# One step of a two-graph pipeline reordered on three engines, and one add moved in the closing

## The chip, the cores and the metric

The kernel runs on one core of one Trainium2 chip. The metric is device microseconds of one execution; times quoted for a kernel are the median of several executions.

## The reference

One layer of a gated graph network on 64 graphs of 128 nodes with 256 features, in float32:

```
mask[d]  = (adj == d),  d = 1..4                 # adj holds 0 and 1 here
agg[d]   = mask[d] / (rowsum(mask[d]) + 1e-8) @ hid
out      = relu(concat_d(agg[d]) @ Wd.T + bd)
r        = sigmoid(out @ Wri.T + bri + hid @ Wrh.T + brh)
z        = sigmoid(out @ Wzi.T + bzi + hid @ Wzh.T + bzh)
n        = tanh(out @ Wni.T + bni + r * (hid @ Wnh.T + bnh))
o        = (1 - z) * n + z * hid
result   = (o - mean(o)) / sqrt(var(o) + 1e-5) * gamma + beta
```

## The kernel before, in words

The 64 graphs are worked in 32 pairs, numbered from 0. Step i does the label sums (y, p and t banks) of pair i, the gates of pairs i-2 and i-3, and the normalisation of pair i-4. Steps 0 and 1 are `head()`, step 2 and step 3 are written out (`plain_step()` and `step()`), and from step 4 on every step is `fast_step()`, in which the products y = x Wd are also done with seven block products instead of eight (A.. and S.. are blocks of x and their sums, B.. and T.. blocks of the weights). Step 4 is the first of these, `n == 1`, with its own branches; it works on the fifth pair, number 4, and prepares the x of the sixth, number 5. Behind step 31 each engine has a `tail()`, the closing.

Every float32 operand of TensorE is split in a high part, rounded by ScalarE (`x_hi`, `y_hi`, `o_hi`), and a rest, taken by GpSimd or VectorE (`x_lo`, `y_lo`, `o_lo`), and a product is three passes. Each engine has its own program, written out by hand; an engine works its rows in that order and waits at semaphores (`wait_ge`). So an instruction that waits holds up all that stands behind it on its engine.

The path of a pair's x: a DMA on SyncE's queue (`load_x`, L316) brings it into `x_f`, GpSimd adds and subtracts four sum blocks (`sum_blocks`, three instructions, L1729, L1731 and L1735, which count `xsum_ready` up), ScalarE rounds all eight blocks to `x_hi` (L1013 in a fast step), and GpSimd takes `x_lo` (L1848).

What stands around the change in step 4:

- TensorE: the products of y: A11 B11, S2 T2, A12 B21, S3 T3 and S1 T1, then A22 T4 (it waits for `u3y_ready`), then S4 B22 (it waits for `y22_ready`), then the gate products. The counts of labels (`counted`, L438, eight tiny matmuls) stand at the end of step 3 for pair 4, and from step 5 on between S1 T1 and A22 T4.
- ScalarE: copies `u2_y` out of the bank (L1007), rounds x (L1013), rounds `y_hi` (L1017), copies `u3_y` (L1021), takes the sigmoid of r (L1026; it waits for `result_ready`, the last row of VectorE's normalisation), and so on to `gamma` (L1040), the bias of the next gate product.
- GpSimd: at the end of step 3 `o_lo` (L1787), then the two rows of the root 1/sqrt(var + eps) (L1827, L1829), then, at the start of step 4, the sums of pair 5.
- VectorE: L1410 adds up the mix, L1465 takes the rest of weight block T4, L1476 (two rows) scales and shifts with the root (`rstd_ready`), L1480 takes a `y_lo`, L1484 adds `u3_y` and counts `y22_ready` up.

In the closing VectorE centres the mix (`centre`, L1546) and then adds C12 (L1647, `c12_ready`), for which ScalarE's next `gamma` waits (L1116); TensorE's product S1 T1 of the closing waits for that `gamma` and for GpSimd's `o_lo` (L1905).

Of the kernel before, what the change touches and what calls it, by code (L numbers as in the profile page):

```python
# [4 lines left out]
GRAPHS, N, H, D = 64, 128, 256, 4  # L5
# [7 lines left out]
XRING = 4  # L13
# [25 lines left out]
def gnn_kernel(nc, x, xT, adjT, wdT, wgT, bd, vectors, out):  # L39
    f32, f32r, bf16, i32 = mybir.dt.float32, mybir.dt.float32r, mybir.dt.bfloat16, mybir.dt.int32  # L40
    ALU, ACT = mybir.AluOpType, mybir.ActivationFunctionType

    ctx = ExitStack()
    with ctx:
# [29 lines left out]
        x_f = sb("x_f", [128, 2, 8, N])  # L74
        x_hi = sb("x_hi", [128, XRING, 8, N], f32r)
# [100 lines left out]
        xhi_ready = sem("xhi_ready")  # L176
        xlo0_ready = sem("xlo0_ready")
        xlo_ready = sem("xlo_ready")
        xsum_ready = sem("xsum_ready")
# [107 lines left out]
        def has_pair(k):  # L287
            return 0 <= k < PAIRS
# [119 lines left out]
        def _(pe):  # L408
# [25 lines left out]
            def counted(k):  # L434
                for g in range(2):
                    halves = masks[:, k % 2, g, :, :].bitcast(bf16).rearrange("n d (m t) -> n d m t", t=2)
                    for d in range(D):
                        last = nc.tensor.matmul(t_bank[:, g * D + d:g * D + d + 1], halves[:, d, :, 1],  # L438
                                                ones_bf[:, :], start=True, stop=True)
                last.then_inc(count_done, 1)  # L440
# [90 lines left out]
            def step(i, up):  # L531
# [11 lines left out]
                def count(k):  # L543

                    pe.wait_ge(masks_ready, up(D * (k + 1), D))
                    pe.wait_ge(olo_ready, up(k - 1))
                    counted(k)
# [91 lines left out]
                pe.wait_ge(c22_ready, up(q + 1))  # L639
                product(gamma, S4, B22).then_inc(p3_done, 1)  # L640
                p_part(i, 1, False)
                count(i + 1)

            def fast_step(i, up):

                q, n, slot = i - LAG_GATES, i - YS + 1, i % XRING

                def y_product(dst, left, w, first=False):
                    return three_passes(dst[:, :], x_hi[:, slot, left, :], x_lo[:, slot, left, :], *wd_block(w), first=first)

                def product(k, dst, left, w):
                    three_passes(dst[:, 0:GATE], x_hi[:, k % XRING, left, :], x_lo[:, k % XRING, left, :],
                                 wx_hi[:, w, :], wx_lo[:, w, :])
                    return three_passes(dst[:, 128:512], o_hi[:, k % 2, left - 1, :], o_lo[:, k % 2, left - 1, :],
                                        wo_hi[:, w, :], wo_lo[:, w, :])

                pe.wait_ge(xlo_ready, up(i - 1))

                if n == 1:
                    pe.wait_ge(ylo_ready[0], 2 * YS)  # L660
                else:
                    pe.wait_ge(yl21_ready, up(n - 1))
                y_product(y_alpha, A11, B11, True).then_inc(yp1_done, 1)
                if n == 1:
                    pe.wait_ge(alpha_loaded, up(q + 1))
                    pe.wait_ge(olo_ready, up(q + 1))
                    product(q, alpha, A11, B11).then_inc(p1_done, 1)
                else:

                    pe.wait_ge(u3_ready, up(q - 1))  # L670
                    product(q - 1, alpha, A22, T4).then_inc(p4_done, 1)
                    pe.wait_ge(yl11_ready, up(n - 1))
                    pe.wait_ge(yl12_ready, up(n - 1))
                    pe.wait_ge(out_ready, up(2 * i - 1, 2))
                    p_products(i - 1, 1, False)
                pe.wait_ge(y11_seeded, up(n))
                if n == 1:
                    pe.wait_ge(wdt_ready, 3)
                y_product(y_alpha, S2, T2).then_inc(yp6_done, 1)
                if n >= 2:  # L680
                    pe.wait_ge(c22_ready, up(q))
                    product(q - 1, gamma, S4, B22).then_inc(p3_done, 1)
                y_product(beta, A12, B21).then_inc(yp2_done, 1)
                pe.wait_ge(p_scaled, up(4 * i, 4))
                p_products(i - 1, 1, True)
                pe.wait_ge(u2y_ready, up(n))
                y_product(y_alpha, S3, T3).then_inc(yp7_done, 1)
                if n == 1:
                    pe.wait_ge(ylo_ready[1], 2 * YS)
                else:  # L690
                    pe.wait_ge(y12_ready, up(n - 1))
                y_product(y_gamma, S1, T1, True).then_inc(yp5_done, 1)
                if n >= 2:
                    pe.wait_ge(alpha_loaded, up(q + 1))
                    pe.wait_ge(olo_ready, up(q + 1))
                    product(q, alpha, A11, B11).then_inc(p1_done, 1)
                    pe.wait_ge(masks_ready, up(D * (i + 1), D))
                    counted(i)
                pe.wait_ge(u3y_ready, up(n))
                if n == 1:  # L700
                    pe.wait_ge(wdt_ready, 4)
                y_product(y_alpha, A22, T4).then_inc(yp4_done, 1)
                pe.wait_ge(y22_ready, up(n))
                y_product(y_gamma, S4, B22).then_inc(yp3_done, 1)
                pe.wait_ge(beta_seeded, up(q + 1))
                pe.wait_ge(oslo_ready, up(q))
                product(q, alpha, S2, T2).then_inc(p6_done, 1)
                pe.wait_ge(out_ready, up(2 * i, 2))
                pe.wait_ge(ratio_ready, up(i + 1))
                transposes()  # L710
                pe.wait_ge(gamma_loaded, up(q + 1))
                product(q, gamma, S1, T1).then_inc(p5_done, 1)
                pe.wait_ge(yl21_ready, up(n))
                pe.wait_ge(yl22_ready, up(n))
                p_products(i, 0, False)
                pe.wait_ge(u2_ready, up(q))
                product(q, alpha, S3, T3).then_inc(p7_done, 1)
                product(q, beta, A12, B21).then_inc(p2_done, 1)
                pe.wait_ge(p_scaled, up(4 * i + 2, 4))
                p_products(i, 0, True)  # L720
# [65 lines left out]
        def _(act):  # L786
# [189 lines left out]
            def fast_step(i, up):  # L976
                q, m, n = i - LAG_GATES, i - LAG_MIX, i - YS + 1

                def scale(k, g):
# [3 lines left out]
                    for b in range(2):  # L983
                        nc.scalar.activation(p_bank[:, b * H:(b + 1) * H], p_bank[:, b * H:(b + 1) * H], ACT.Copy,  # L984
                                             scale=ratio[:, k % 2, g, b:b + 1]).then_inc(p_scaled, 1)

                if n == 1:

                    act.wait_ge(wdt_sum, 4)
                    act.wait_ge(y_done[1], 2 * YS)  # L990
                    nc.scalar.activation(wd_block(T4)[0], wd_sum_of[T4], ACT.Copy).then_inc(wdt_hi_ready, 1)
# [13 lines left out]
                if n >= 2:  # L1005
                    act.wait_ge(yl12_ready, up(n - 1))
                nc.scalar.activation(u2_y[:, :], y_alpha[:, :], ACT.Copy).then_inc(u2y_ready, 1)  # L1007
                if has_pair(i + 1):
                    k = i + 1
                    act.wait_ge(xsum_ready, up(3 * k, 3))  # L1010

                    act.wait_ge(p3_done, up(i - 2))
                    nc.scalar.activation(x_hi[:, k % XRING, :, :], x_f[:, k % 2, :, :], ACT.Copy).then_inc(xhi_ready, 1)  # L1013
                act.wait_ge(yp2_done, up(n))

                act.wait_ge(p_done, up(2 * i, 2))
# [2 lines left out]
                if n >= 2:  # L1019
                    act.wait_ge(yl22_ready, up(n - 1))  # L1020
                nc.scalar.activation(u3_y[:, :], y_alpha[:, :], ACT.Copy).then_inc(u3y_ready, 1)  # L1021
                act.wait_ge(c11_ready, up(m + 1))
                act.wait_ge(c21_ready, up(m + 1))

# [149 lines left out]
        def _(dve):  # L1174
# [366 lines left out]
            def tail():  # L1541
                last = PAIRS - 1

                def centre(k, g):
                    dve.wait_ge(mv_ready, 2 * k + 2)
                    nc.vector.scalar_tensor_tensor(mix[:, g * H:(g + 1) * H], mix[:, g * H:(g + 1) * H],  # L1546
                                                   mean_var[:, g, 0:1], vec_rows[:, gamma_rows],
                                                   ALU.subtract, ALU.mult).then_inc(scaled_ready, 1)
# [91 lines left out]

                mixed(last - 3)
                moments(last - 3)
                centre(last - 3, 0)
                centre(last - 3, 1)
                dve.wait_ge(p3_done, last - 1)
                dve.wait_ge(u2_ready, last - 2)
                nc.vector.tensor_tensor(c_sb[:, ODD, 1, :], gamma[:, :], u2_sb[:, :], ALU.add).then_inc(c12_ready, 1)  # L1647
                sum_labels(1)

                dve.wait_ge(y12_ready, YPAIRS)  # L1650
# [59 lines left out]
        def _(pool):  # L1710
# [65 lines left out]
            def step(i, up):  # L1776
# [13 lines left out]
                if i == HEAD:  # L1790
# [32 lines left out]
                                        from_n[:, :].rearrange("p (g f) -> p g f", g=2), ALU.mult)\  # L1823
                    .then_inc(zpart_ready, 1)
                split_o_sums()
                pool.wait_ge(mv_ready, 2)
                nc.gpsimd.tensor_tensor(var_eps[:, :], mean_var[:, :, 1], ln_eps[:, :], ALU.add).then_inc(ve_ready, 1)  # L1827
                pool.wait_ge(ve_ready, 1)
# [1 line left out]

            def fast_step(i, up):
                m, j, n = i - LAG_MIX, i - LAG_NORM, i - YS + 1
                if n == 1:
                    sum_blocks(i + 1, up, 16 * ((i + 1) // 2 + 1))
                if n >= 2:
                    pool.wait_ge(mv_ready, up(2 * j + 2, 2))
                    nc.gpsimd.tensor_tensor(var_eps[:, :], mean_var[:, :, 1], ln_eps[:, :], ALU.add).then_inc(ve_ready, 1)  # L1837
# [127 lines left out]
```

## Time and profile before

| | us |
|---|---|
| median of 3 executions (510.44 to 510.72) | 510.55 |
| the profiled execution, its own time | 512.22 |
| its span, first to last instruction | 510.4 |
| TensorE busy (96% of the span) | 492.4 |
| VectorE busy (84%) | 429.1 |
| ScalarE busy (83%) | 421.9 |
| GpSimd busy (73%) | 370.4 |
| an x_f load, issue to landing, median | 2.6 |

The views name engines PE (TensorE), ACT (ScalarE), DVE (VectorE), POOL (GpSimd) and SPq (the DMA queue of SyncE). TensorE is busy in nearly the whole span, so what counts is where it stands still and at which clock it works; the mean granted clock is 0.988 of full speed.

### The profile page before, as it was taken

Reading aid. Unit: us, or ns where it says so; the run is one execution under the profiler, and the core shown is the slowest. Engines: PE = TensorE matmul, PEld = TensorE weight load, DVE = VectorE, ACT = ScalarE, POOL = GpSimd, SP = SyncE. Lnnn points to the kernel's source line nnn. Section 1 sums busy time; section 2 is a strip of 40 time slices with the busy share of each in tenths; the row PEclk is TensorE's granted clock in tenths of the full one; section 3 lists DMA queues with packets and bytes.
Section 4 is the critical chain, followed back from the end, with each engine's and each line's share of the span. In section 5 each row is a group of like instructions: output and inputs, shape, how many; then the busy total and the mean of one; then the engine's idle time right before and its main releaser. Section 6 shows DMA issues by size and latency. Waiting matters only on the chain.

```text
span 510.4 us, 10652 instructions
## 1 busy us (share of the span) xinstructions
PE 492.4 (96%) x2951; PEld 447.7 (88%) x2951; DVE 429.1 (84%) x1077; ACT 421.9 (83%) x819; POOL 370.4 (73%) x369
## 2 busy tenths in 40 slices
PE   8999979999999999999999999999999999999992
PEld 4789769999999999999999999999999999999892
DVE  4899968888888988888898888889888888988877
ACT  5878758888888898888989888888988889897772
POOL 2889776777887777788777778877777887775535
PEclk9999979999999999999999999999999999999997
DMA  8310222111222212122221212222111222110111
GB/s 274 127 54 1 83 83 73 53 51 44 74 74 72 72 51 51 41 72 72 72 72 51 51 41 72 72 72 72 51 51 41 72 72 72 51 41 22 42 42 62
DMA packets 20261, 33.42 MB, mean 65 GB/s; under 512 B 2256, under 2 KB 6992, under 8 KB 20240
## 3 DMA queue, kind: packets, MB, share of 16 engines
q1 hardware_dynamic: 19872, 32.38, 20.4%
q10 hardware_dynamic: 288, 0.52, 0.3%
q0 software_dynamic: 80, 0.26, 0.1%
q8 instruction: 9, 0.15, 0.1%
q14 instruction: 12, 0.10, 0.1%
HBM read 24.77 MB, written 8.39 MB: 65 GB/s over the span
## 4 chain that ended last, share of the span: by engine, by line
PE 86%; POOL 6%; DVE 4%; issue 1%; DMA 1%; ACT 1%; SPq 0%; POOLq 0%; ACTq 0%; DVEq 0%
PE y_bank L412 25%; PE alpha L412 24%; PE gamma L412 12%; PE p_bank L449 11%; PE beta L412 10%; PE t_bank L457 3%; DMA adj_in<-in_adjT 1%; PE t_bank L438 1%; POOL x_lo L1782 1%; POOL wo_lo L1739 1%; DVE y_lo L1203 1%; POOL x_rows L1743 1%; POOL x_f L1731 0%; DVE wd_lo L1209 0%; DVE mix L1410 0%
## 5 line engine op out<-in xcount | busy, mean ns | idle before, releaser
L449 PE MATMUL p_bank<-y_hi,masks 128*128 128x256 f32 x256 | 66.9, 283 | 1.1 <-DVE y_lo L1203 0.4
L449 PE MATMUL p_bank<-y_lo,masks 128*128 128x256 f32 x256 | 66.5, 282 | 0.0
L1848 POOL TENSOR_TENSOR x_lo<-x_f,x_hi 128x1024 fp32r<-128x1024 f32 x27 | 65.1, 2410 | 1.2 <-ACT x_hi L1013 1.2
L1851 POOL TENSOR_TENSOR y_lo<-shared,y_hi 128x512 fp32r<-128x512 f32 x28 | 36.6, 1309 | 25.2 <-ACT y_hi L1036 25.2
L1837 POOL TENSOR_TENSOR var_eps<-mean_var,ln_eps 128x2 f32<-128x2 f32 x27 | 5.3, 196 | 66.2 <-DVE mean_var L1455 66.2
L449 PEld LDWEIGHTS p_bank<-y_hi,masks 128*128 128x128 f32 x256 | 48.1, 188 | 4.4 <-issue 1.4
L412 PE MATMUL y_bank<-wd_hi,x_hi 128*128 128x512 f32 x112 | 47.2, 422 | 3.3 <-ACT shared L1021 3.3
L449 PEld LDWEIGHTS p_bank<-y_lo,masks 128*128 128x128 f32 x256 | 48.2, 188 | 1.3
L984 ACT ACTIVATE p_bank<-p_bank,ratio 128x256 f32<-128x256 f32 x112 | 45.3, 448 | 0.3 <-PE p_bank L449 0.3
L412 PE MATMUL y_bank<-wd_lo,x_hi 128*128 128x512 f32 x112 | 44.8, 400 | 0.0
L412 PE MATMUL y_bank<-wd_hi,x_lo 128*128 128x512 f32 x112 | 44.6, 398 | 0.0
L412 PE MATMUL alpha<-wx_hi,x_hi 128*128 128x384 f32 x122 | 41.4, 339 | 0.1
L412 PE MATMUL alpha<-wx_hi,x_lo 128*128 128x384 f32 x122 | 41.4, 340 | 0.0
L412 PE MATMUL alpha<-wo_hi,o_hi 128*128 128x384 f32 x122 | 41.4, 339 | 0.0
L412 PE MATMUL alpha<-wo_hi,o_lo 128*128 128x384 f32 x122 | 41.4, 339 | 0.0
L412 PE MATMUL alpha<-wx_lo,x_hi 128*128 128x384 f32 x122 | 41.2, 338 | 0.0
L412 PE MATMUL alpha<-wo_lo,o_hi 128*128 128x384 f32 x122 | 41.2, 337 | 0.0
L1859 POOL TENSOR_TENSOR shared<-x_rows,shared 128x512 f32<-128x512 f32 x28 | 36.3, 1295 | 3.8 <-ACT shared L1045 3.8
L1426 DVE SCALAR_TENSOR_TENSOR out_rows<-p_bank,rcount,bd_rows 128x256 f32<-128x256 f32 x56 | 27.1, 483 | 13.3 <-PE p_bank L449 11.5
L1863 POOL TENSOR_TENSOR shared<-shared 128x512 f32<-128x512 f32 x28 | 36.2, 1295 | 2.2
L1866 POOL TENSOR_TENSOR y_lo<-shared,y_hi 128x512 fp32r<-128x512 f32 x28 | 36.6, 1309 | 0.0
L1843 POOL TENSOR_TENSOR o_lo<-o_sums,o_hi 128x512 fp32r<-128x512 f32 x27 | 35.0, 1297 | 0.0
(315 smaller groups left out, 1796.2 us busy)
## 6 DMA issues: line engine op xcount, KB each, us to landing
x_f<-in_xT SPq DMA_DIRECT2D x32, 256.0 KB, 2.6
x_rows<-in_x SPq DMA_DIRECT2D x32, 256.0 KB, 2.7
out<-shared SPq DMA_DIRECT2D x31, 256.0 KB, 2.0
adj_in<-in_adjT SPq DMA_DIRECT2D x32, 128.0 KB, 2.1
shared<-in_wgT SPq DMA_DIRECT2D x2, 576.0 KB, 6.6
shared<-in_wdT ACTq DMA_DIRECT2D x2, 256.0 KB, 5.4
vec_rows<-in_vectors SPq DMA_DIRECT2D x1, 512.0 KB, 7.0
shared<-in_wgT SPq DMA_DIRECT2D x2, 192.0 KB, 7.8
```

The lines of the kernel that those rows point to most:

```text
L412: done = nc.tensor.matmul(dst, m, w, start=(first and t == 0), stop=(last and t == 2), skip_group_check=inside)
L449: last = nc.tensor.matmul(p_bank[:, b * H:(b + 1) * H], masks[:, k % 2, g, d, :], part[:, g, d * H:(d + 1) * H], start=first, stop=(part i ...
L457: last = nc.tensor.transpose(t_bank[:, (2 * g + c) * N:(2 * g + c + 1) * N], out_rows[:, g, c * N:(c + 1) * N], ident[:, :])
L984: nc.scalar.activation(p_bank[:, b * H:(b + 1) * H], p_bank[:, b * H:(b + 1) * H], ACT.Copy, scale=ratio[:, k % 2, g, b:b + 1]).then_inc(p ...
L1426: nc.vector.scalar_tensor_tensor(out_rows[:, g, :], p_bank[:, 0:H], rcount[:, k % 2, g, 1:2], bd_rows[:, :], ALU.mult, ALU.add).then_inc(h ...
L1837: nc.gpsimd.tensor_tensor(var_eps[:, :], mean_var[:, :, 1], ln_eps[:, :], ALU.add).then_inc(ve_ready, 1)
L1843: nc.gpsimd.tensor_tensor(*split_lo(o_lo[:, i % 2, 3:7, :], o_sums[:, 1:5, :], o_hi[:, i % 2, 3:7, :]))\
L1848: nc.gpsimd.tensor_tensor(*split_lo(x_lo[:, k % XRING, :, :], x_f[:, k % 2, :, :], x_hi[:, k % XRING, :, :])).then_inc(xlo_ready, 1)
L1851: nc.gpsimd.tensor_tensor(*split_lo(y_lo[:, EVEN, half(1)], u3_y[:, :], y_hi[:, EVEN, half(1)]))\
L1859: nc.gpsimd.tensor_tensor(from_n[:, :], x_rows[:, m % 2, :, :].rearrange("p g f -> p (g f)"), n_sb[:, :], ALU.subtract).then_inc(from_read ...
L1863: nc.gpsimd.tensor_tensor(z_part[:, :].rearrange("p (g f) -> p g f", g=2), rz_sb[:, :, 1, :], from_n[:, :].rearrange("p (g f) -> p g f", g ...
L1866: nc.gpsimd.tensor_tensor(*split_lo(y_lo[:, ODD, half(1)], u2_y[:, :], y_hi[:, ODD, half(1)]))\
```

## The change

In step 4 four things move. ScalarE rounds the x of pair 5 behind the copy to `u3_y` instead of behind the copy to `u2_y`. GpSimd makes the sums of pair 5 at the end of step 3, ahead of the two rows of the root, instead of at the start of step 4 behind them, and waits for the same load (48 is what the formula before gives). TensorE counts the labels of pair 4 between S1 T1 and A22 T4 of step 4 instead of at the end of step 3, as all later steps do, and the wait for `olo_ready` that stood ahead of that count goes. In the closing VectorE adds C12 ahead of the two centring rows. No instruction is added or taken out.

```diff
 # TensorE, step() (step 3)
                 p_part(i, 1, False)
-                count(i + 1)
 # TensorE, fast_step()
-                    pe.wait_ge(masks_ready, up(D * (i + 1), D))
-                    counted(i)
+                pe.wait_ge(masks_ready, up(D * (i + 1), D))
+                counted(i)
                 pe.wait_ge(u3y_ready, up(n))
 # ScalarE, fast_step()
+                def x_high():
+                    k = i + 1
+                    act.wait_ge(xsum_ready, up(3 * k, 3))
+
+                    act.wait_ge(p3_done, up(i - 2))
+                    nc.scalar.activation(x_hi[:, k % XRING, :, :], x_f[:, k % 2, :, :], ACT.Copy).then_inc(xhi_ready, 1)
...
                 nc.scalar.activation(u2_y[:, :], y_alpha[:, :], ACT.Copy).then_inc(u2y_ready, 1)
-                if has_pair(i + 1):
-                    k = i + 1
-                    act.wait_ge(xsum_ready, up(3 * k, 3))
-
-                    act.wait_ge(p3_done, up(i - 2))
-                    nc.scalar.activation(x_hi[:, k % XRING, :, :], x_f[:, k % 2, :, :], ACT.Copy).then_inc(xhi_ready, 1)
+                if n >= 2 and has_pair(i + 1):
+                    x_high()
...
                 nc.scalar.activation(u3_y[:, :], y_alpha[:, :], ACT.Copy).then_inc(u3y_ready, 1)
+                if n == 1:
+
+                    x_high()
 # VectorE, tail()
-                centre(last - 3, 0)
-                centre(last - 3, 1)
                 dve.wait_ge(p3_done, last - 1)
                 dve.wait_ge(u2_ready, last - 2)
                 nc.vector.tensor_tensor(c_sb[:, ODD, 1, :], gamma[:, :], u2_sb[:, :], ALU.add).then_inc(c12_ready, 1)
+                centre(last - 3, 0)
+                centre(last - 3, 1)
 # GpSimd, step() (step 3)
                 split_o_sums()
+
+                sum_blocks(5, up, 48)
                 pool.wait_ge(mv_ready, 2)
 # GpSimd, fast_step()
-                if n == 1:
-                    sum_blocks(i + 1, up, 16 * ((i + 1) // 2 + 1))
```

ScalarE's rows of step 4 before, from the copy to `u2_y` (first row) over the rounding of x (second) and the copy to `u3_y` (fourth):

```order
L1007 ACTIVATE shared<-y_bank 128x512
L1013 ACTIVATE x_hi<-x_f 128x1024
L1017 ACTIVATE y_hi<-beta 128x512
L1021 ACTIVATE shared<-y_bank 128x512
L1026 ACTIVATE mix<-shared 128x512
```

The same stretch of the changed kernel, whose lines have other numbers:

```order
L1013 ACTIVATE shared<-y_bank 128x512
L1019 ACTIVATE y_hi<-beta 128x512
L1023 ACTIVATE shared<-y_bank 128x512
L991 ACTIVATE x_hi<-x_f 128x1024
L1031 ACTIVATE mix<-shared 128x512
```

The rounding of x now stands behind the copy to `u3_y` and ahead of the sigmoid of r.

GpSimd's rows at the seam of steps 3 and 4 before: `o_lo`, the two rows of the root, the three rows of the sums of pair 5, and the rest `x_lo` of pair 5:

```order
L1787 TENSOR_TENSOR o_lo<-o_sums,o_hi 128x512
L1827 TENSOR_TENSOR var_eps<-mean_var,ln_eps 128x2
L1829 TENSOR_TENSOR rstd<-var_eps,power 128x2
L1729 TENSOR_TENSOR x_f<-x_f 128x128
L1731 TENSOR_TENSOR x_f<-x_f 128x256
L1735 TENSOR_TENSOR x_f<-x_f 128x128
L1848 TENSOR_TENSOR x_lo<-x_f,x_hi 128x1024
```

The same stretch of the changed kernel:

```order
L1792 TENSOR_TENSOR o_lo<-o_sums,o_hi 128x512
L1734 TENSOR_TENSOR x_f<-x_f 128x128
L1736 TENSOR_TENSOR x_f<-x_f 128x256
L1740 TENSOR_TENSOR x_f<-x_f 128x128
L1834 TENSOR_TENSOR var_eps<-mean_var,ln_eps 128x2
L1836 TENSOR_TENSOR rstd<-var_eps,power 128x2
L1853 TENSOR_TENSOR x_lo<-x_f,x_hi 128x1024
```

The root is now behind the three sums, and `x_lo` is behind the root as before.

On TensorE the difference is one row, the count of pair 4, at the seam of steps 3 and 4 and at its new place in step 4, between S1 T1 (weights `wdt`) and A22 T4 (weights `wd`):

```order
 L449 MATMUL p_bank<-y_lo,masks 128x256
-L438 MATMUL t_bank<-ones_bf,masks 128x1 x8
 L412 MATMUL y_bank<-wd_hi,x_hi 128x512
 L412 MATMUL y_bank<-wd_hi,x_lo 128x512
@@ -282,4 +281,5 @@
 L412 MATMUL y_bank<-wdt_hi,x_lo 128x512
 L412 MATMUL y_bank<-wdt_lo,x_hi 128x512
+L438 MATMUL t_bank<-ones_bf,masks 128x1 x8
 L412 MATMUL y_bank<-wd_hi,x_hi 128x512
 L412 MATMUL y_bank<-wd_hi,x_lo 128x512
```

All other rows of TensorE keep their order.

## Rows read from the trace of the kernel before

**Rows 1.** Waits of TensorE, whole execution: total us, times, longest.

```profile
PE y_bank L412 <- ACT shared L1021: 3.3, 1, 3.3
PE gamma L412 <- POOL o_lo L1905: 0.6, 1, 0.6
```

**Rows 2.** Windows: length, busy us by engine (PE PEld DVE ACT POOL), granted clock, DMA.

```profile
94.00:109.00 15.00, 15.00 (x93) 13.85 (x92) 12.86 (x34) 13.05 (x26) 11.36 (x12) 1.00 0.21 62
67.00:68.00 1.00, 0.00 (x0) 0.00 (x0) 0.00 (x0) 1.00 (x2) 0.01 (x1) 0.97 0.89 260
```

**Rows 3.** Timeline of TensorE, step 4: start, us, form [idle before <- releaser].

```profile
59.87 0.34 PE L438 MATMUL t_bank<-ones_bf,masks 128*128 128x1 bf16 x8 [0.84 <-DVE o_lo L1350]
...
61.09 0.44 PE L412 MATMUL alpha<-wx_hi,x_hi 128*128 128x384 f32 x1
...
64.57 0.39 PE L412 MATMUL y_bank<-wdt_lo,x_hi 128*128 128x512 f32 x1
...
68.94 0.79 PE L412 MATMUL y_bank<-wd_hi,x_hi 128*128 128x512 f32 x1 [3.27 <-ACT shared L1021]
...
70.38 0.63 PE L412 MATMUL y_bank<-wd_hi,x_hi 128*128 128x512 f32 x1
...
78.69 0.39 PE L412 MATMUL y_bank<-wd_hi,x_hi 128*128 128x512 f32 x1
```

**Rows 4.** Timeline of ScalarE, steps 3 and 4.

```profile
60.44 0.60 ACT L974 ACTIVATE alpha<-vec_rows 128x512 f32<-128x512 f32 x1
...
66.85 1.06 ACT L1013 ACTIVATE x_hi<-x_f 128x1024 fp32r<-128x1024 f32 x1 [3.11 <-POOL x_f L1735]
...
68.29 0.59 ACT L1021 ACTIVATE shared<-y_bank 128x512 f32<-128x512 f32 x1
68.77 0.60 ACT L1026 ACTIVATE mix<-shared 128x512 f32<-128x512 f32 x1
...
71.32 0.60 ACT L1040 ACTIVATE gamma<-bias_step 128x512 f32<-128x512 f32 x1
```

**Rows 5.** Timeline of GpSimd at the seam of steps 3 and 4.

```profile
60.73 1.29 POOL L1787 TENSOR_TENSOR o_lo<-o_sums,o_hi 128x512 fp32r<-128x512 f32 x1
63.73 0.19 POOL L1827 TENSOR_TENSOR var_eps<-mean_var,ln_eps 128x2 f32<-128x2 f32 x1 [1.72 <-DVE mean_var L1320]
64.00 0.72 POOL L1829 TENSOR_TENSOR rstd<-var_eps,power 128x2 f32<-128x2 f32 x1
...
66.36 0.46 POOL L1735 TENSOR_TENSOR x_f<-x_f 128x128 f32<-128x128 f32 x1
```

**Rows 6.** Timeline of TensorE, step 5 and the start of step 6.

```profile
87.26 0.39 PE L412 MATMUL y_bank<-wd_hi,x_hi 128*128 128x512 f32 x1
...
89.37 0.42 PE L412 MATMUL gamma<-wx_hi,x_hi 128*128 128x384 f32 x1
...
93.56 0.39 PE L412 MATMUL y_bank<-wd_hi,x_hi 128*128 128x512 f32 x1
```

**Rows 7.** Timeline of VectorE, steps 4 and 5.

```profile
60.80 1.77 DVE L1410 TENSOR_TENSOR mix<-shared 128x512 f32<-128x512 f32 x1 [1.09 <-POOL shared L1822]
...
64.99 0.71 DVE L1465 TENSOR_TENSOR wd_lo<-x_rows,wd_hi 128x512 fp32r<-128x512 f32 x1
...
66.02 0.86 DVE L1476 SCALAR_TENSOR_TENSOR shared<-mix,rstd,vec_rows 128x256 f32<-128x256 f32 x2
...
84.42 0.86 DVE L1476 SCALAR_TENSOR_TENSOR shared<-mix,rstd,vec_rows 128x256 f32<-128x256 f32 x2
...
85.80 0.68 DVE L1484 TENSOR_TENSOR shared<-y_bank,shared 128x512 f32<-128x512 f32 x1
```

**Rows 8.** Timeline of SyncE's queue, steps 3 and 4: the load of pair 5.

```profile
52.35 0.44 SPq L316 DMA_DIRECT2D x_f<-in_xT x1
```

**Rows 9.** Timelines of ScalarE and GpSimd in the closing.

```profile
484.31 0.60 ACT L1116 ACTIVATE gamma<-bias_step 128x512 f32<-128x512 f32 x1 [1.15 <-DVE shared L1647]
483.78 1.28 POOL L1905 TENSOR_TENSOR o_lo<-o_sums,o_hi 128x512 fp32r<-128x512 f32 x1
```

## The prediction

> **What bounds the kernel now.** I read the waits of TensorE first, then the windows, then the timelines of step 4. TensorE is the bound: in a stretch of 15 us behind step 4 it is busy all 15.00 us at full clock, while VectorE (12.86), ScalarE (13.05) and GpSimd (11.36) have room [rows 2]. So time can only be won where TensorE stands still or works at the low clock. The view of waits has one large entry, 3.3 us in one piece: a product into `y_bank` waits for ScalarE's copy to `u3_y`, L1021 [rows 1]. The timeline places it: A22 T4 starts at 68.94 behind 3.27 us of idle time, so the last matmul of S1 T1 had ended at 65.67 [rows 3].
>
> Why it waits is seen on two queues. ScalarE had stood idle for 3.11 us ahead of the rounding of x (L1013, at 66.85), released by GpSimd's last sum of pair 5, L1735; the copy to `u3_y` is queued behind that rounding and starts at 68.29 [rows 4]. GpSimd ended `o_lo` at 60.73 + 1.29 = 62.02, then stood still 1.72 us for the means, made the two rows of the root, 63.73 to 64.72, and only then the sums, to 66.36 + 0.46 = 66.82 [rows 5]. So sums that needed nothing of the root stood behind it, and a copy that needed nothing of the sums behind them.
>
> The stop has a second cost. The granted clock of 67 to 68 us is 0.97, which at two levels (full is 2.4 GHz, half is 1.2 GHz) means that it fell to half at about 67.94, when TensorE had been idle for 2.3 us [rows 2]; the matmul at 68.94 shows 0.79 us where its like shows 0.39 [rows 3, 6]. From the first matmul of S4 B22 to the first of the next step TensorE took 78.69 - 70.38 = 8.31 us in step 4 [rows 3] and 93.56 - 87.26 = 6.30 us in step 5, the same work in the same order [rows 6]: 2.01 us of low clock behind S4 alone.
>
> **The change part by part.** I follow step 4 as it should now run, and ask each time what is late next.
>
> TensorE, count. The wait of 0.84 us ahead of the count at 59.87 goes [rows 3], and A11 B11 of y can start about 1 us earlier, this wait and the count itself. This gains nothing: the next product, alpha, needs the bias copy L974, which ends at 60.44 + 0.60 = 61.04, and alpha started at 61.09 already [rows 3, 4]. ScalarE's rows up to there use results of step 3 and not this count, so I leave alpha at 61.09 and the products up to S1 T1 where they are; the idle time ahead of the count becomes idle time ahead of alpha, which should be 61.09 - (59.87 - 0.84 + 0.7) = 1.4 us, with 0.7 for A11 B11's three passes. At its new place the count takes about 0.2 to 0.3 us (its own row shows 0.34 with its drain), in a gap, as will be seen: cost nothing. If that gap were closed it would cost these 0.3.
>
> ScalarE. The copy to `u3_y` needs S3 T3, whose last matmul starts at 64.57 and ends at 64.96 [rows 3]. The copy takes 0.59 [rows 4], so `u3_y` is there at 65.6 instead of 68.88. The rounding of x, 1.06, follows to about 66.6; it is covered, since the sigmoid of r behind it waits for VectorE's last normalised row, not there before 66.88.
>
> GpSimd. Sums and root took 63.73 to 66.82, 3.09 us, in the old order [rows 5]. Started at 62.02 they end at 65.1. VectorE's mix add L1410 shows what may disturb: it started at 60.80 and lasted 1.77, to 62.57, which is 0.55 after GpSimd's `o_lo` ended [rows 7, 5]. If the first sum has to wait for that end, the pair ends at 62.57 + 3.09 = 65.7. In both cases the root is there before VectorE wants it at 66.02 [rows 7]; its slack is 0.3 to 0.9, where before it was 66.02 - 64.72 = 1.3. The sums end about 0.99 sooner, 64.1 to 64.7, in time for ScalarE at 65.6.
>
> VectorE is what is late next. A22 T4 can start at about 65.9, when the count and `u3_y` are through and L1465, the rest of T4's weights (64.99 + 0.71 = 65.70), is there; it takes three passes, 0.7 us, half of the 70.38 - 68.94 = 1.44 that it took at the half clock [rows 3]. Then S4 B22 waits for `y22_ready`, L1484. That row could not run before L1476, which starts at 66.02 behind rows that do not move. In step 5, where nothing holds this stretch up, L1484 ends at 85.80 + 0.68 = 86.48, 2.06 us after the start of L1476 at 84.42 [rows 7]. So it ends at 66.02 + 2.06 = 68.08, and S4 B22 starts at 68.14 (0.06 from the end of `u3_y`, 68.88, to the matmul at 68.94). A new stop of about 1.5 us takes the place of the old one.
>
> One thing can push this. The power row of the root, 0.72, now ends between 65.1 and 65.7, across the start of L1465 at 64.99. If VectorE has to wait for it, L1465 ends up to 0.55 after 65.7, at 66.25 instead of 65.70 [rows 5, 7]: 0 to 0.55 later for all behind it. I take 0.2, nearer the low end, since GpSimd's rows of pair 5 in the old order lay across L1465 too and it lasted 0.71 only. The Trainium skill, SBUF — State Buffer, section Who interferes with whom, says that a VectorE instruction with two SBUF inputs and a GpSimd instruction that reads SBUF cannot run together, the later one waits to the other's end. The 0.55 of L1410 behind `o_lo` agrees with it; by it S4 B22 would start near 68.4, which lies within the bounds taken here.
>
> So S4 B22 starts at 68.14 + 0.2 = 68.34 (bounds 68.14 and 68.69) instead of 70.38. Behind it ScalarE has to keep up: `gamma` ended at 71.32 + 0.60, that is 3.15 us after the sigmoid of r started at 68.77 [rows 4]. With the sigmoid at 66.95 + 0.2 it is there at 70.3; TensorE wants it 89.37 - 87.26 = 2.11 after S4 B22 [rows 6], at 70.45. That holds, by 0.15. With step 5's 6.30 us the next step starts at 68.34 + 6.30 = 74.64 instead of 78.69: **4.05 us earlier** (bounds 74.44 and 74.99, gains 4.25 and 3.70). From there on TensorE is the bound, and the whole rest moves.
>
> Closing. C12 ahead of centring brings `gamma` L1116, which ended at 484.91, forward by the 0.8 us of the two centring rows. TensorE's product also waits for GpSimd's `o_lo`, which ends at 483.78 + 1.28 = 485.06, and the view of waits names that as the releaser [rows 9, 1]. Nothing moves it: its queue waits for means and roots ahead of the centring. Gain 0, at most the 0.1 between the two ends if the releaser is misread. The centring rows are 0.7 late, and the first to use them stands behind the closing's label sums: cost 0.
>
> **Sum.** Against the profiled execution: span 510.4 - 4.05 = 506.35, its own time 512.22 - 4.05 = 508.2. Its own time lies 1.67 above the median of the executions shown, which I take as the same offset for both kernels, so the prediction is 510.55 - 4.05 = 506.5.
>
> **The rivals.**
> 1. A further small wait in steps 4 or 5, because three queues now follow closely: `gamma` with 0.15 us to spare, and behind it GpSimd with `x_lo` and the y rests. Each would cost tenths, together up to 1 us: 506.8 to 507.5. Against it speaks that each queue has 2 to 3.6 us of room in a step of this length [rows 2]. 1 in 10.
> 2. The clock falls again. Two stops remain, 1.4 us ahead of alpha and 1.5 us ahead of S4 B22. The old fall came at 2.3 us of idle time, the 0.84 us stop left no trace. If it fell all the same, the stretch behind S4 loses its 2.0 us again, with T4's share up to 2.9: 508.5 to 509.4. 6 in 100.
> 3. Slower: GpSimd's sums now stand ahead of the root, so a late load of pair 5 would hold up the root, then VectorE's L1476, then all. The load was issued at 52.35 [rows 8], and loads land after 2.6 us in the median, 7 us ahead of 62.02. The root has at least 0.3 us of slack; to eat the gain of 4.05 it would have to be over 4.3 us late, the load then landing after about 66.3 and thus 14 us after its issue. Price: each us beyond that one us. 2 in 100, 511 to 513.
> 4. No change: the gain is swallowed later by another bound. The windows show none, TensorE alone is at 100%. 2 in 100.
>
> The forecast has 8 in 10. Its own bounds give 506.3 to 506.85. The range takes in rival 1 and 0.4 us below for a row of VectorE that comes sooner than I think or a bank that comes free earlier: 505.9 to 507.6. What a measurement can tell from no change is about 0.2%, 1.0 us; rivals 1 and 2 and the forecast all lie beyond that. Faster 0.96, same 0.02, slower 0.02.
>
> **What would show it.** In the profile after, the 3.3 us entry of `y_bank` waiting for ScalarE's `u3_y` copy is gone, and in its place stands one of about 1.5 us where S4 B22 waits for VectorE's L1484 (another line number). Ahead of alpha a wait of 1.4 us for ScalarE's bias copy appears and the count's wait for `o_lo` is gone. The granted clock stays 1.00 in step 4, all of the span's mean near 1.0. S4 B22 starts near 68.3, step 5 near 74.6. GpSimd's root ends near 65.1 to 65.7. The wait in the closing for GpSimd's `o_lo` is still 0.6. I am wrong if VectorE's L1476 starts well after 66.02, if ScalarE's rounding of x runs beyond the release of the sigmoid, or if the clock in step 4 shows half again.

## The result, and the profile after

The changed kernel takes 508.06 us in the median of 4 executions (507.51 to 508.24), the kernel before beside it 510.63 us (4 executions, 510.44 to 511.29). The ratio is 0.9946, with a 95% interval of 0.9931 to 0.9961: faster by 2.6 us, where 4.05 was forecast. 508.06 lies outside the range of 505.9 to 507.6.

The profiled execution tells another story. Its own time is 508.01 us and its span 506.2, where the profiled execution of before had 512.22 and 510.4: 4.2 us less, close to the forecast 508.2 and 506.35. Step 4 did what the prediction says, and what is off lies between a profiled execution and a median.

The waits of TensorE in the changed kernel (total us, times, longest; compare [rows 1]):

```profile
PE alpha L412 <- ACT alpha L973: 1.4, 1, 1.4
PE y_bank L412 <- DVE shared L1489: 1.4, 1, 1.4
...
PE gamma L412 <- POOL o_lo L1910: 0.6, 1, 0.6
```

The 3.3 us behind ScalarE's copy is gone. Two stops of 1.4 us have come, one ahead of alpha and one ahead of S4 B22, which waits for VectorE's `y22_ready` (now L1489). The 0.6 us in the closing stays. The timeline of TensorE shows where they lie (start, us, form, idle before; compare [rows 3]):

```profile
60.99 0.44 PE L412 MATMUL alpha<-wx_hi,x_hi 128*128 128x384 f32 x1 [1.37 <-ACT alpha L973]
...
65.42 0.35 PE L438 MATMUL t_bank<-ones_bf,masks 128*128 128x1 bf16 x8
65.70 0.47 PE L412 MATMUL y_bank<-wd_hi,x_hi 128*128 128x512 f32 x1
...
67.98 0.50 PE L412 MATMUL y_bank<-wd_hi,x_hi 128*128 128x512 f32 x1 [1.35 <-DVE shared L1489]
...
70.18 0.42 PE L412 MATMUL gamma<-wx_hi,x_hi 128*128 128x384 f32 x1
...
74.36 0.39 PE L412 MATMUL y_bank<-wd_hi,x_hi 128*128 128x512 f32 x1
```

A22 T4 starts at 65.70 instead of 68.94, S4 B22 at 67.98 instead of 70.38 (68.34 forecast), and step 5 at 74.36 instead of 78.69 (74.64 forecast). The granted clock is at full speed in every window from 58 to 80 us, two of which are (length, TensorE's busy time, clock, DMA share, GB/s; compare [rows 2]):

```profile
67.00:68.00 1.00, 0.02 (x1) 1.00 0.91 346
68.00:69.00 1.00, 1.00 (x5) 1.00 0.25 88
```

The three queues that the prediction followed, in the changed kernel. ScalarE (compare [rows 4]), the copy to `u3_y` first:

```profile
64.92 0.60 ACT L1023 ACTIVATE shared<-y_bank 128x512 f32<-128x512 f32 x1
65.41 1.05 ACT L991 ACTIVATE x_hi<-x_f 128x1024 fp32r<-128x1024 f32 x1
66.84 0.60 ACT L1031 ACTIVATE mix<-shared 128x512 f32<-128x512 f32 x1 [0.38 <-DVE shared L1481]
...
69.41 0.59 ACT L1045 ACTIVATE gamma<-bias_step 128x512 f32<-128x512 f32 x1
```

GpSimd, sums first and root behind (compare [rows 5]):

```profile
60.61 1.28 POOL L1792 TENSOR_TENSOR o_lo<-o_sums,o_hi 128x512 fp32r<-128x512 f32 x1
61.86 0.91 POOL L1734 TENSOR_TENSOR x_f<-x_f 128x128 f32<-128x128 f32 x1
...
64.35 0.72 POOL L1836 TENSOR_TENSOR rstd<-var_eps,power 128x2 f32<-128x2 f32 x1
```

VectorE (compare [rows 7]):

```profile
60.68 1.77 DVE L1415 TENSOR_TENSOR mix<-shared 128x512 f32<-128x512 f32 x1 [1.06 <-POOL shared L1827]
...
64.87 0.68 DVE L1470 TENSOR_TENSOR wd_lo<-x_rows,wd_hi 128x512 fp32r<-128x512 f32 x1
...
65.87 0.86 DVE L1481 SCALAR_TENSOR_TENSOR shared<-mix,rstd,vec_rows 128x256 f32<-128x256 f32 x2
...
67.25 0.68 DVE L1489 TENSOR_TENSOR shared<-y_bank,shared 128x512 f32<-128x512 f32 x1
```

The root ends at 65.07, 0.8 us before VectorE's L1481 starts. VectorE's row L1489 ends at 67.93, and S4 B22 follows at 67.98. The closing (compare [rows 9]), first ScalarE, then GpSimd:

```profile
479.60 0.60 ACT L1121 ACTIVATE gamma<-bias_step 128x512 f32<-128x512 f32 x1 [0.66 <-DVE shared L1650]
...
479.55 1.28 POOL L1910 TENSOR_TENSOR o_lo<-o_sums,o_hi 128x512 fp32r<-128x512 f32 x1
```

`gamma` is there at 480.20, `o_lo` at 480.83, and TensorE goes on at 480.98.

### The profile page after: what moved, and what is told of

Read it like the earlier page. It is cut to its first block, busy times and chain, and to the rows that moved or that the text cites. A ratio compares the mean times of both kernels' runs of the same rounds, so it can differ in the third digit from the quotient of the medians.

```text
span 506.2 us, 10651 instructions
## 1 busy us (share of the span) xinstructions
PE 489.2 (97%) x2951; PEld 444.8 (88%) x2951; DVE 429.2 (85%) x1077; ACT 421.7 (83%) x819; POOL 369.9 (73%) x369
## 4 chain that ended last, share of the span: by engine, by line
PE 86%; POOL 5%; DVE 5%; issue 2%; DMA 1%; ACT 0%; SPq 0%; POOLq 0%; ACTq 0%; DVEq 0%
PE y_bank L412 25%; PE alpha L412 24%; PE gamma L412 12%; PE p_bank L449 11%; PE beta L412 10%; PE t_bank L457 3%; DMA adj_in<-in_adjT 1%; PE t_bank L438 1%; POOL x_lo L1787 1%; POOL wo_lo L1744 1%; DVE y_lo L1208 1%; POOL x_rows L1748 1%; DVE wd_lo L1214 0%; DVE mix L1415 0%; DVE masks L1183 0%
```

## The experiments

All times are medians of executions, with their range and number; the ratio is to the kernel before, run beside them on the same chip. The profiled execution of each kernel also gives the distance from alpha's first matmul to step 5's first in TensorE's timeline. This distance is the better measure of the seam: alpha's own start varies from 60.38 to 61.09 us between profiled executions of these kernels (run 10, which moves it, apart), from causes ahead of it.

**Runs 1 and 2: is the low clock of step 4 always there?** The kernel before, unchanged, with more executions:

> The kernel before, unchanged, for the times, spans and mean clocks of many executions. Theory A (the length of the low-clock stretch behind the 3.3 us stop differs from execution to execution, and the profiled one of 512.22 us had a long one): executions spread from about 510.4 to 512.3 us, span 1.8 us below the time in each, and the longer ones have the lower mean clock, by 0.003 for each 1.7 us. Theory B (the profiled execution was 1.67 us longer by an offset of profiling that all profiled executions have): executions within 0.3 us of one another with equal clocks, and profiled ones above.

Measured: 510.45 us (509.33 to 513.16, 12), ratio 0.9994 [0.9979, 1.001]. In each execution the time is the span and 1.8 us, so nothing lies around the span that differs. What differs is the clock: the mean granted clock of an execution ranges from 0.984 to 0.993. Over the 75 executions of the kernel before that were timed in these experiments, the ten at 0.993 took 509.12 to 510.22 us, the eleven at 0.988 took 511.26 to 512.97, and the two at 0.984 took 513.16 and 513.32. In between the time does not follow the mean clock closely: those at 0.990 and 0.991 lie from 509.29 to 511.51. The profiled execution of this run, 511.09, is one among the others, so being profiled adds no offset. TensorE's timeline and windows in it:

```profile
60.86 0.44 PE L412 MATMUL alpha<-wx_hi,x_hi 128*128 128x384 f32 x1
...
68.73 0.50 PE L412 MATMUL y_bank<-wd_hi,x_hi 128*128 128x512 f32 x1 [3.27 <-ACT shared L1021]
...
77.53 0.39 PE L412 MATMUL y_bank<-wd_hi,x_hi 128*128 128x512 f32 x1
```

```profile
69.00:70.00 1.00, 1.00 (x5) 0.99 0.02 4
70.00:71.00 1.00, 1.00 (x4) 0.50 0.00 0
...
73.00:74.00 1.00, 1.00 (x8) 0.80 0.00 0
```

At two levels, 0.99 in the row at 69 to 70 and 0.80 in the row at 73 to 74 say that the low stretch reached from 69.98 to 73.40, 3.4 us. In the profiled execution that the prediction was made from, it began at 67.94 [rows 2], and this window puts its end at 74.76, so it was 6.8 us long:

```profile
74.00:75.00 1.00, 1.00 (x6) 0.62 0.00 0
```

The stop is the same in both, 3.27 us. The distance from alpha to step 5 is 16.67 us here and was 78.69 - 61.09 = 17.60 there [rows 3].

The second run keeps TensorE occupied in the long stop, with matmuls of zeros into a bank that is overwritten afterwards (added work, nothing left out; ScalarE's `gamma` of step 4 waits for their end, which is not shown here):

```diff
+                if n == 1:
+                    pe.wait_ge(c12_ready, 2)
+                    for _ in range(13):
+                        filler = nc.tensor.matmul(gamma[:, :], zeros_bf[:, 0:128], zeros_bf[:, :], start=True, stop=True)
+                    filler.then_inc(filled, 1)
                 pe.wait_ge(u3y_ready, up(n))
...
```

> The kernel before with 13 zero matmuls of 512 columns in TensorE's 3.3 us stop of step 4, ahead of the wait for the copy to u3_y, into a free bank; 13 x 0.22 = 2.9 us, so they end before the wait does. They take no idle time away, only keep TensorE at work. Theory A: the clock stays full, the stretch behind S4 B22 takes 6.3 us and not 8.3, S4 B22 starts at 69.8; span 507.8, time 509.6, and the scatter of before is gone. Theory B: 2.6 us below the unprofiled median, 508.0. If the clock falls in spite of the matmuls (they are zeros) time stays at 510.6.

Measured: 509.5 us (509.23 to 509.92, 12), ratio 0.9972 [0.996, 0.9983]. TensorE's timeline, in which one of the 13 matmuls has left no record, and two of its windows:

```profile
61.01 0.44 PE L413 MATMUL alpha<-wx_hi,x_hi 128*128 128x384 f32 x1
...
65.67 2.75 PE L703 MATMUL gamma<-zeros_bf 128*128 128x512 bf16 x12
68.86 0.50 PE L413 MATMUL y_bank<-wd_hi,x_hi 128*128 128x512 f32 x1 [0.43 <-ACT shared L1027]
...
69.69 0.50 PE L413 MATMUL y_bank<-wd_hi,x_hi 128*128 128x512 f32 x1
...
76.12 0.39 PE L413 MATMUL y_bank<-wd_hi,x_hi 128*128 128x512 f32 x1
```

```profile
67.00:68.00 1.00, 1.00 (x6) 1.00 0.90 318
70.00:71.00 1.00, 1.00 (x6) 1.00 0.00 0
```

The copy to `u3_y` comes as late as ever, but every window of step 4 shows full clock, and alpha to step 5 is 15.11 us. So this is the kernel before with the low clock taken out: 17.60 - 15.11 = 2.5 us of low clock in the execution that I predicted from, and 16.67 - 15.11 = 1.6 in that of run 1. Against all 75 executions of the kernel before (median 510.84, 509.12 to 513.32), the low clock costs the median 510.84 - 509.5 = 1.3 us. The spread of single executions narrows from 3.8 us in run 1 to 0.7. By the mean clock and the time, the ten executions at 0.993 (median 509.7) lost next to nothing to the low clock although they had the same order of work; none of them was traced.

**Runs 3 to 6: which part of the change does it?** GpSimd's move alone, all else as before:

```diff
                 split_o_sums()
+                sum_blocks(5, up, 48)
                 pool.wait_ge(mv_ready, 2)
...
-                if n == 1:
-                    sum_blocks(i + 1, up, 16 * ((i + 1) // 2 + 1))
```

> The kernel before with GpSimd's move alone (sums of pair 5 ahead of the root). Theory S (the sums behind the root were the cause, ScalarE's order does not matter once they are early): the rounding of x runs at about 64.1 to 65.2, the copy to u3_y ends at 66.3, A22 T4 starts there, and S4 B22 waits for VectorE's add near 68.0 as in the changed kernel; time 508.1, the same as the changed kernel within 0.3. Rival (both moves are needed): the stop for u3_y stays above 1 us and is passed on, time 508.8 or more.

Measured: 507.57 us (507.44 to 507.91, 6), ratio 0.9938 [0.9922, 0.9954]. The whole gain is there. What is left of the 3.3 us falls into two pieces in TensorE's timeline, alpha first:

```profile
60.59 0.44 PE L412 MATMUL alpha<-wx_hi,x_hi 128*128 128x384 f32 x1
...
65.86 0.51 PE L412 MATMUL y_bank<-wd_hi,x_hi 128*128 128x512 f32 x1 [0.68 <-ACT shared L1021]
67.58 0.50 PE L412 MATMUL y_bank<-wd_hi,x_hi 128*128 128x512 f32 x1 [0.76 <-DVE shared L1484]
```

With alpha at 60.59, S4 B22 is 6.99 us behind it, as in the changed kernel (67.98 - 60.99 = 6.99). The 0.68 us that ScalarE's rounding still costs A22 T4 only shortens the wait for VectorE behind it.

ScalarE's move alone:

```diff
                 nc.scalar.activation(u3_y[:, :], y_alpha[:, :], ACT.Copy).then_inc(u3y_ready, 1)
+                if n == 1:
+                    k = i + 1
+                    act.wait_ge(xsum_ready, up(3 * k, 3))
+                    act.wait_ge(p3_done, up(i - 2))
+                    nc.scalar.activation(x_hi[:, k % XRING, :, :], x_f[:, k % 2, :, :], ACT.Copy).then_inc(xhi_ready, 1)
```

> The kernel before with ScalarE's move alone (x of pair 5 rounded behind the copy to u3_y). Theory S: the rounding still waits for the sums until 66.8 and now holds up the sigmoid of r and all behind it: sigmoid at 67.9, gamma ready at 71.0 where TensorE wants it at 70.2, so 0.8 us behind the changed kernel, 508.9. Rival (the copy to u3_y was all that mattered): the same as the changed kernel, 508.1.

Measured: 508.93 us (508.41 to 509.67, 9), ratio 0.9965 [0.9952, 0.9978]. The sums still come late, so the rounding, now ahead of the sigmoid, holds that up. ScalarE's timeline, and TensorE's in the fence behind it:

```profile
66.52 1.06 ACT L1027 ACTIVATE x_hi<-x_f 128x1024 fp32r<-128x1024 f32 x1 [1.26 <-POOL x_f L1741]
```

```profile
60.74 0.44 PE L412 MATMUL alpha<-wx_hi,x_hi 128*128 128x384 f32 x1
...
67.78 0.51 PE L412 MATMUL y_bank<-wd_hi,x_hi 128*128 128x512 f32 x1 [1.35 <-DVE shared L1490]
...
69.16 0.44 PE L412 MATMUL alpha<-wx_hi,x_hi 128*128 128x384 f32 x1 [0.40 <-ACT beta L1040]
...
74.88 0.39 PE L412 MATMUL y_bank<-wd_hi,x_hi 128*128 128x512 f32 x1
```

The time was forecast right. The wait showed at `beta`, the copy behind the sigmoid, and not at `gamma`. Alpha to step 5 is 14.14 us, against 13.37 in the changed kernel. So ScalarE's move alone takes about 2 us off the kernel before, most of the gain, by letting the copy to `u3_y` pass the late sums.

Both moves together (the diffs of runs 3 and 4), with count and closing as before:

> The kernel before with GpSimd's and ScalarE's moves, the count of labels and the closing as before. Its stops in step 4 are 0.85 us ahead of the count and about 1.35 us ahead of S4 B22, so one long stop where the changed kernel has two and GpSimd's move alone has none above 0.85. Median 507.7; by theory C executions at 509 with a mean clock of 0.991 are fewer than in the changed kernel, but may be there.

Measured: 507.72 us (507.51 to 507.75, 5), ratio 0.9936 [0.9922, 0.9949], alpha to step 5 13.40 us. Since run 3 had come out below the changed kernel, GpSimd's move alone was run once more:

> GpSimd's move alone again, for more executions beside the changed kernel on the same chip. Its stops are 0.85, 0.7 and 0.8 us. Theory C: no execution with a fallen clock, all between 507.4 and 508.0, median 507.6, so 0.3 to 0.5 us below the changed kernel. Rival (its lower median of the first time was chance): executions at 509 as often as in the changed kernel.

Measured: 508.04 us (507.69 to 508.48, 5), ratio 0.9944 [0.9931, 0.9958]. The expected lead of 0.3 to 0.5 us did not come back. GpSimd's move alone (11 executions, median 507.78), both moves, and the whole change (17 executions, median 508.00) are one result within what can be told here.

**Runs 7 to 9: the changed kernel again, and its closing.**

> The changed kernel again, for the times, spans and mean clocks of many executions. Theory A (nothing in it lets the clock fall in the work, so its time is the predicted span of 506.2 plus 1.8): 508.0, all executions within 0.7 us, mean clock 0.993 to 0.995 in every one, while the kernel before spreads over 4 us beside it.

Measured: 508.07 us (507.39 to 509.2, 8), ratio 0.995 [0.9929, 0.997]. The executions were expected close together. Two of the eight, 509.05 and 509.20, were not, both with a mean clock of 0.991, and one of them is the profiled one. Its windows and its timeline of TensorE:

```profile
60.00:61.00 1.00, 0.28 (x1) 0.95 0.20 67
61.00:62.00 1.00, 1.00 (x4) 0.50 0.02 8
...
64.00:65.00 1.00, 1.00 (x6) 0.84 0.00 0
```

```profile
60.72 0.56 PE L412 MATMUL alpha<-wx_hi,x_hi 128*128 128x384 f32 x1 [1.38 <-ACT alpha L973]
...
68.01 0.50 PE L412 MATMUL y_bank<-wd_hi,x_hi 128*128 128x512 f32 x1 [0.16 <-DVE shared L1489]
...
75.03 0.39 PE L412 MATMUL y_bank<-wd_hi,x_hi 128*128 128x512 f32 x1
```

The clock fell at about 60.9, 0.2 us after TensorE had begun again behind the 1.38 us stop ahead of alpha, and came back at about 64.3. Step 5 starts 75.03 - 60.72 = 14.31 us after alpha, 0.94 later than 13.37. TensorE was busy through these 3.4 us, which is 1.7 us of work lost by an estimate from the two levels, but S4 B22 now waits 0.16 us instead of 1.35: the second stop took up most of it. S4 B22 is only 0.30 us late against alpha (68.01 - 60.72 = 7.29, where it was 6.99); the other 0.64 lie behind it, 0.34 of them in a new wait for ScalarE's `beta`. A later repeat:

> The changed kernel again, beside the others of this call: median 508.0, and about one execution in four at 509 to 509.5 with a mean clock of 0.991, the rest at 507.4 to 508.3 with 0.993 or more.

Measured: 507.75 us (507.44 to 508.11, 5), ratio 0.9939 [0.9926, 0.9953], with none of the five above 508.2. So 2 of 17 executions of the changed kernel were slowed so, the one seen in a trace and the other told by its mean clock. One in four had been expected.

The changed kernel with the closing as before (C12 behind the two centring rows again):

```diff
+                centre(last - 3, 0)
+                centre(last - 3, 1)
                 dve.wait_ge(p3_done, last - 1)
                 dve.wait_ge(u2_ready, last - 2)
                 nc.vector.tensor_tensor(c_sb[:, ODD, 1, :], gamma[:, :], u2_sb[:, :], ALU.add).then_inc(c12_ready, 1)
-                centre(last - 3, 0)
-                centre(last - 3, 1)
```

> The changed kernel with the closing as it was (centring ahead of C12). By the prediction's step the closing's product waits for GpSimd's o_lo in both orders: the same as the changed kernel within 0.2 us, and its wait in the closing still 0.6. Rival (gamma was the last to come): 0.3 to 0.6 us slower.

Measured: 507.96 us (507.52 to 509.3, 9), ratio 0.9942 [0.9924, 0.996]. TensorE still waits 0.6 us for GpSimd's `o_lo`. The closing's edit is worth nothing that can be measured. One of the nine executions, 509.30, again has a mean clock of 0.991.

**Runs 10 to 12: can the two remaining stops be won?** In the changed kernel, ScalarE copies alpha's bias ahead of rounding the sums in step 3, so that alpha need not wait:

```diff
                 evict(ODD, 0, beta, c11_ready)
-                round_sums()
                 act.wait_ge(p4_done, 2)
                 evict(EVEN, 0, alpha, c21_ready)
                 act.wait_ge(c21_ready, 2)
                 nc.scalar.activation(alpha[:, :], vec_rows[:, 0:512], ACT.Copy).then_inc(alpha_loaded, 1)
+                round_sums()
```

> The changed kernel with ScalarE's eviction and new bias of alpha in step 3 ahead of its rounding of the o sums, which waits for VectorE. The bias is there at 58.8 and not 60.9, so TensorE's first remaining stop (1.37 us ahead of alpha) goes. Theory V (VectorE's row for y22 sets when S4 B22 starts): S4 B22 still starts near 68.0, the stops ahead of A22 T4 and S4 B22 grow by the 1.3 us, and the time is that of the changed kernel within 0.2. Rival (TensorE's own work is the bound of step 4): 1.3 us faster, 506.7. If the longer stops let the clock fall: up to 2.9 us slower in some executions.

Measured: 508.35 us (507.5 to 511.27, 12), ratio 0.9962 [0.9943, 0.998]. TensorE's timeline:

```profile
59.59 0.41 PE L412 MATMUL alpha<-wx_hi,x_hi 128*128 128x384 f32 x1 [0.15 <-DVE o_lo L1355]
...
65.56 0.47 PE L412 MATMUL y_bank<-wd_hi,x_hi 128*128 128x512 f32 x1 [1.12 <-DVE wd_lo L1470]
...
67.84 0.50 PE L412 MATMUL y_bank<-wd_hi,x_hi 128*128 128x512 f32 x1 [1.36 <-DVE shared L1489]
```

The stop went from ahead of alpha to ahead of A22 T4 and nothing was gained: VectorE sets when S4 B22 may start. Of the 12 executions 5 have a mean clock of 0.991 or less, the longest of them 511.27 us at 0.989, where the changed kernel had 2 of 17. Two stops closer together may let the clock fall more often, but with these counts chance is not excluded, and none of the five was traced.

Then VectorE's two y rows of step 4 ahead of its two scaling rows (this changes the order of work only; the rows themselves are wrapped in two functions, not shown here):

```diff
...
+                for part in ((y_rows, scaled_rows) if n == 1 else (scaled_rows, y_rows)):
+                    part()
```

> The changed kernel with VectorE's two y rows of step 4 (the rest of y11, and the add that S4 B22 waits for) ahead of its two scaling rows. S4 B22 starts at 67.1 and not 68.0. Theory V alone: 0.85 us faster, 507.2. Theory W (ScalarE follows as closely: its sigmoid of r waits for the scaling rows, now 1.1 us later, and the bias copy for S2 T2 is behind it): S2 T2 starts at 69.65 and not 68.8, time 0.9 us slower, 508.9.

Measured: 509.62 us (508.6 to 510.87, 12), ratio 0.9979 [0.9965, 0.9994]. S4 B22 no longer waits, but the scaling rows are late for ScalarE's sigmoid, and `beta` for TensorE:

```profile
68.44 0.60 ACT L1031 ACTIVATE mix<-shared 128x512 f32<-128x512 f32 x1 [0.75 <-DVE shared L1482]
```

```profile
70.12 0.44 PE L412 MATMUL alpha<-wx_hi,x_hi 128*128 128x384 f32 x1 [1.55 <-ACT beta L1039]
```

It is 1.6 us slower than the changed kernel where 0.9 was forecast. The profiled execution had a fallen clock from about 60.9 to 64.3 as well (0.94 in the window 60 to 61, 0.85 in 64 to 65), again beginning 0.2 us behind the stop ahead of alpha, which started at 60.68. The six executions with a mean clock of 0.994 or more have a median of 509.27, 1.3 us above the changed kernel, so by this most of the excess comes from the order and not from the clock.

Last, 5 matmuls of zeros in each of the changed kernel's two stops (added work, nothing left out). The edit is that of run 2, at two places:

> The changed kernel with 5 zero matmuls of 512 columns in each of TensorE's two remaining stops of step 4 (1.37 us ahead of alpha, 1.35 us ahead of S4 B22), 1.1 us each, so that they end before what the stop waits for. Theory C (the executions of the changed kernel with a mean clock of 0.991 and 509.1 us are those in which the clock fell in one of these stops): all executions between 507.4 and 508.3, none with a mean clock of 0.991 or less, median 507.9. If the clock falls elsewhere, some executions stay at 509.

Measured: 507.68 us (507.58 to 507.98, 5), ratio 0.9937 [0.9923, 0.9951]. The two stops shrink to 0.28 and 0.25 us and alpha to step 5 is 13.41. The median is that of the changed kernel. The five executions lie within 0.4 us, but so do those of runs without zeros, so whether they prevent the rare fall is not shown by five. No version beat the changed kernel by more than can be told.

## Why the prediction was right in its steps on the engines and wrong in its number

**Right.**

- The reading of the stop. GpSimd's sums behind the root, ScalarE's rounding behind the sums, and TensorE behind ScalarE: run 3 moves the sums alone and the 3.3 us stop is gone.
- What is late next: VectorE's last normalised row and `y22_ready`. L1481 starts at 65.87 and L1489 ends 2.06 us later, at 67.93, the 2.06 us that were taken from step 5 [rows 7].
- The waits of 1.4 ahead of alpha and about 1.5 ahead of S4 B22, measured 1.37 and 1.35.
- `gamma` in time by 0.15 us: it ends at 70.00 and TensorE starts on it at 70.18.
- The closing and the count at nothing. `gamma`'s bias copy did end earlier, at 480.20, but `o_lo`, 479.55 + 1.28 = 480.83, was the last, as [rows 9] say. C12 did not gain the full 0.8 us in its place either: the row itself then waited 0.33 us for TensorE.
- The 4.05 us, as a statement on the profiled execution: step 5 starts 4.33 us earlier. S4 B22 came 0.36 sooner than forecast (0.20 taken for the power row, 0.15 because VectorE's L1481 started at 65.87 and not 66.02), and from there to step 5 it took 74.36 - 67.98 = 6.38 instead of 6.30.

**A term that was mis-sized.** I let the power row hold VectorE's L1465 up by 0.2 us, with bounds of 0 and 0.55. It was 0: L1470 ran from 64.87 and took 0.68 us, with the power row running from 64.35 to 65.07. The first sum, 128x128, was held: 0.91 us at 61.86 where its like takes 0.46 [rows 5], ending 0.3 after VectorE's L1415. The rule of the Trainium skill, SBUF — State Buffer, section Who interferes with whom, that a VectorE instruction with two SBUF inputs and a GpSimd instruction that reads SBUF shut each other out, fits this first sum and `o_lo`. It does not fit the power row, which ran 0.2 us into L1470 (64.87 to 65.07) without lengthening it.

**The step that failed** is the last sentence of the sum: "Its own time lies 1.67 above the median of the executions shown, which I take as the same offset for both kernels". It was no offset of being profiled. The time is 1.8 us above the span in profiled and unprofiled executions alike. Those 1.67 us were mostly low clock beyond that of the median execution (2.5 us lost to it against 1.3), a stretch of 6.8 us where run 1's profile has 3.4, and low clock in step 4 is what the change takes away. So I counted a gain of 2.0 us behind S4 and 0.7 in T4 [rows 3, 6] from a median that had lost only half of it. What the runs give in its place:

- idle time: S4 B22 starts 69.69 - 61.01 = 8.68 us behind alpha in run 2 and 6.99 in the changed kernel, 1.7 us;
- low clock: 1.3 us in the median execution of before, by run 2;
- together 3.0 us, against 510.84 - 508.00 = 2.8 in the pooled medians and 2.6 in the first comparison. In the profiled execution it was 1.7 and 2.5, the 4.2 that the two profiles show.

Worked out the safe way, from a full-clock step 4, the forecast would have been 509.5 - 1.7 = 507.8. That needs run 2. With what there was before, the way to it was the disagreement itself: 512.22 stood beside a median of 510.55, with a granted clock of 0.988 that could have been below that of the others, and I did not count that as a case.

**Rival 2** did occur, at another place and price. I wrote that the clock fell at 2.3 us of idle time, and that two shorter stops would most likely leave it up. It fell 0.2 us behind the end of a 1.4 us stop in the trace of run 7 (and in that of run 11, which has the same stop), and by the mean clock in 2 of 17 executions of the changed kernel, at a price of 1 us where I had 2.0 to 2.9. The median does not see it. Rivals 1, 3 and 4 did not occur in the changed kernel's first profile.

## What to carry to other kernels

When the profiled execution lies apart from the median, find out what differs (mean clock first, then span) before a gain is read off it, and forecast from the part that every execution has: here the idle time was certain and half the clock's share was not. Put the row that needs nothing ahead of the one that waits, and then expect the next queue to be the bound: of a 3.3 us stop 1.35 stayed, and two attempts to remove what remained only moved it. In a change of several parts run each alone; here one moved call, GpSimd's, gave all of the gain, and the others added nothing to it that can be measured, although ScalarE's move gave about 2 us where it stood alone. Two moves that cure the same stop do not add up.

## What the runs showed of the hardware that was not expected

- The same stop of 3.27 us was followed by 3.4 us at the 1.2 GHz level in one execution and 6.8 in another. In the one the clock fell within the stop, at 67.94; in the other at 69.98, 1.25 us after TensorE had begun again at 68.73. What sets the length is open. With TensorE kept at work in the stop (run 2), the spread of 3.8 us fell to 0.7, so most of the spread of the kernel before hangs on it; its longest executions, 513.2 and 513.3, were not traced.
- The clock can fall just behind a stop of 1.4 us, 0.2 us after TensorE had begun again (traces of runs 7 and 11); by the mean clock it did so in 2 of 17 executions of the changed kernel. With two stops closer together it was 5 of 12, which chance may explain.
- Matmuls of zeros held the clock at its 2.4 GHz level through a stop of 3.3 us, and took the kernel before to 509.5 us from 510.45 in run 1 and 510.93 beside it, although they compute nothing.
- GpSimd's 128x2 power row (64.35 to 65.07) did not hold up a 128x512 VectorE row with two SBUF inputs (from 64.87, 0.68 us), where VectorE's 128x512 mix add beside its `o_lo` took 1.77 us, and like rows 0.68.
